# Matmuls of ones ahead of the first projections, other places for one head's key rotation and for weight splits, and another bank for the fourth query

## The reference, cut to what matters

```
x = x + fake_quant(layernorm(x)) @ fake_quant(ctx)            # layer 0, mixing by the context
x = x + mx_ffn(layernorm(x))      # weights rounded to 4 bits, activations to 6, shared exponents per 32
h = layernorm(x)
q = rope(h @ wq)  (32 heads of 128);  k = rope(ctx @ wk), v = ctx @ wv  (8 heads of 128)
x = x + softmax(q k^T / sqrt(128) + mask) v @ wo              # layer 1, attention
x = x + (silu(g * gate(h2)) * u * up(h2)) @ down * d,  h2 = layernorm(x)
```

## Time and profile before

| what | value |
|---|---|
| median of 3 runs | 683.79 us |
| profiled execution: own time / span in the profile | 685.39 us / 683.6 us |
| PE busy, share of the span | 661.1 us, 97% |
| DVE, POOL, ACT busy | 516.4, 474.2, 347.5 us |
| mean granted TensorE clock | 0.998 |

### The profile page before, as it was taken

One profiled execution on the slowest core, in us unless ns is written; L12 is line 12 of the kernel. 1 busy time (PEld: TensorE's weight loads), 2 busy tenths in 40 slices (PEclk: granted clock), 3 DMA queues, 4 the chain that ended last, 5 costly groups with the idle time before them and its releaser, 6 DMA issues.

```text
span 683.6 us, 10829 instructions
## 1 busy us (share of the span) xinstructions
PE 661.1 (97%) x3004; PEld 486.5 (71%) x3004; DVE 516.4 (76%) x1024; ACT 347.5 (51%) x667; POOL 474.2 (69%) x435
## 2 busy tenths in 40 slices
PE   6999999999899999999999999999999998999997
PEld 2344444446667888888888888888888776888886
DVE  5999897986788888888888888888888886621113
ACT  2686324424656656656666666666556653221111
POOL 0688958334698788787787787797688477076661
PEclk9999999999999999999999999999999999999999
DMA  8999775403322222232231131131233012013311
GB/s 317 390 328 245 230 198 133 155 1 121 94 78 78 63 85 70 61 89 64 61 99 54 61 105 48 61 107 46 61 94 121 17 32 92 1 48 102 111 63 62
DMA packets 59147, 72.63 MB, mean 106 GB/s; under 512 B 23152, under 2 KB 31472, under 8 KB 58096
## 3 DMA queue, kind: packets, MB, share of 16 engines
q1 hardware_dynamic: 59120, 72.31, 34.5%
HBM read 58.00 MB, written 9.44 MB: 99 GB/s over the span
## 4 chain that ended last, share of the span: by engine, by line
PE 67%; DVE 14%; POOL 8%; issue 7%; ACT 2%; DMA 1%; SPq 1%; DVEq 0%; ACTq 0%; POOLq 0%
PE ps L683 14%; PE ps L685 14%; PE ps L684 14%; PE ps L751 10%; PE ps L716 6%; PE ps L568 3%; PE ps L542 3%; POOL mx_raw L1148 2%; DMA mx_raw<-in_mxw 1%; DVE ps L1578 1%; PE ps L604 1%; POOL mx_w L1157 1%; DVE mx_amax L1406 1%; POOL prob L1220 1%; DVE stats L1319 1%
## 5 line engine op out<-in xcount | busy, mean ns | idle before, releaser
L1220 POOL TENSOR_SCALAR prob<-prob,rinv 128x512 f32<-128x512 f32 x128 | 90.0, 703 | 73.6 <-DVE rinv L1585 73.5
L1046 ACT ACTIVATE prob<-ps,nmax 128x512 f32<-128x512 f32 x128 | 88.5, 691 | 97.2 <-DVE nmax L1578 96.8
L751 PE MATMUL ps<-xt,wq_sb 128*128 128x512 f32 x384 | 103.2, 393 | 3.6 <-DVE q_cos L1593 2.1
L1057 ACT CAST pT<-ps 128x512 fp32r<-128x512 f32 x128 | 75.2, 588 | 53.0 <-PE ps L716 51.9
L1578 DVE CUSTOM_DVE_ANT_0 ps<-ps,mask_sb 128x512 f32<-128x512 f32 x128 | 88.0, 687 | 6.6 <-PE ps L685 6.1
L1599 DVE TENSOR_TENSOR pT<-ps,pT 128x512 fp32r<-128x512 f32 x128 | 86.5, 675 | 3.0 <-ACT pT L1057 2.0
L751 PEld LDWEIGHTS ps<-xt,wq_sb 128*128 128x128 f32 x384 | 71.6, 188 | 22.3 <-issue 4.9
L716 PE MATMUL ps<-idf,prob 128*128 128x128 f32 x512 | 76.8, 272 | 0.4 <-POOL prob L1220 0.3
L716 PEld LDWEIGHTS ps<-idf,prob 128*128 128x128 f32 x512 | 63.6, 140 | 17.8 <-POOL prob L1220 1.6
L683 PE MATMUL ps<-pT,vt 128*128 128x512 f32 x128 | 60.8, 475 | 0.6 <-DVE pT L1599 0.5
L542 PE MATMUL ps<-ctxT,wk_sb 128*128 128x512 f32 x128 | 58.0, 594 | 0.4 <-ACT v_st L892 0.4
(11 more groups left out here) (179 smaller groups left out, 1548.0 us busy)
## 6 DMA issues: line engine op xcount, KB each, us to landing
mx_raw<-in_mxw SPq DMA_DIRECT2D x8, 1024.0 KB, 8.1
wq_raw<-in_wq SPq DMA_DIRECT2D x32, 256.0 KB, 3.2
wo_raw<-in_wo SPq DMA_DIRECT2D x32, 256.0 KB, 2.7
v_scr<-v_st SPq DMA_DIRECT2D x16, 256.0 KB, 3.7
k_scr<-k_st SPq DMA_DIRECT2D x16, 256.0 KB, 3.5
kr<-k_scr SPq DMA_DIRECT2D x16, 256.0 KB, 2.8
kr_swp<-k_scr SPq DMA_DIRECT2D x32, 128.0 KB, 3.4
vr<-v_scr SPq DMA_DIRECT2D x16, 256.0 KB, 3.3
```

Of the source, the lines that this page charges most:

```text
L751: last = mm(query_bank(H), wq_sb[:, par, l, k], xt[:, r, k], start=(n == 0), stop=(n == 11))
L1046: nc.scalar.activation(prob[:, j], bank(j % 2), ACT.Exp, bias=nmax[:, j:j + 1], scale=-1.0, accum_out=rsum[:, j:j + 1]).then_inc(exps, 1)
L1057: copy(pT[:, v % 2, 0, :, i * P:(i + 1) * P], bank(2 + i % 2).rearrange("p (k c) -> p k c", k=4)).then_inc(ph_ready, 1)
L1220: nc.gpsimd.tensor_scalar(prob[:, i], prob[:, i], rinv[:, i:i + 1], 1.0, ALU.mult, ALU.mult).then_inc(probs, 1)
```

## The change

Eight matmuls of a tile of ones run on PE as soon as the tile is set, into the bank of the first value unit, ahead of `first_values`. On SP's queue slice 1 goes ahead of the four X transfers and slice 2 ahead of the first mx chunk; the second half of wv goes ahead of the first half of the context rows. On ACT the rounding of the rows goes behind the first two value copies and the two first lifts, and those two copies go ahead of the lifts. Head 0's first rotation moves from the projection stage to POOL's place behind the wait for `inter_ready` 3, the second from there to unit -3; their adds, high and low parts move with them: DVE's first add from between two products to just ahead of `add_down(2)`. Query 3 takes bank 7 rather than bank 6, and queries 3 and 4 wait for one `q_cosed` less. The splits of query weights 2 and 3 go ahead of the query product on POOL. The last key unit's matmuls go one right behind `late_keys(3)` and three at unit -1, rather than two at unit -2 and two at unit -1. In `standardise`, `between` is called right behind the first step.

```diff
+WARM = 8
@@ query_bank
-            return bank(7 if isinstance(head, int) and head == 1 else 6)
+            return bank(7 if isinstance(head, int) and head in (1, 3) else 6)
@@ sync
             slice_load(0)
+            slice_load(1)
             for t in range(NT):
                 sp.dma_start(X[:, t], x[t * P:(t + 1) * P]).then_inc(x_in[t], 16)
-            slice_load(1)
+            slice_load(2)
             mx_load(0)
-            slice_load(2)
             slice_load(3)
...
             sp.dma_start(idf[:], ident).then_inc(id_in, 16)
+            sp.dma_start(wv_sb[:, :, 512:1024], ...).then_inc(wv1_in, 16)
             ctx_load(0)
-            sp.dma_start(wv_sb[:, :, 512:1024], ...).then_inc(wv1_in, 16)
@@ tensor
+            def keep_busy():
+
+                pe.wait_ge(consts_ready, 1)
+                for _ in range(WARM):
+                    mm(bank(rotating(STEPS[0][0][0])), ones[:], ones[:].unsqueeze(1).to_broadcast([P, 4, P]), start=True, stop=True)
+            keep_busy()
             first_values()
...
             late_keys(3, range(2, 4))
+            late_keys(4, range(0, 1))
@@ query
-                    first = isinstance(H, int) and H <= 2
-                    after(pe, q_cosed, H // 2 if first else H)
+                    after(pe, q_cosed, H - 1 if isinstance(H, int) and H <= 4 else H)
@@ unit, PE
-                    if isinstance(U, int) and U in (-2, -1) and j == 3:
-                        late_keys(4, range(2 * U + 4, 2 * U + 6))
+                    if isinstance(U, int) and U == -1 and j == 3:
+                        late_keys(4, range(1, 4))
@@ scalar
             rows_scale()
+            copy_values(0, 0)
+            copy_values(1, 0)
             mx_lift(0, 0)
             mx_lift(0, 1)
-            copy_values(0, 0)
-            copy_values(1, 0)
+            rows_round()
...
+            def first_key_high(b):
+                act.wait_ge(key_roped, b + 1)
+                copy(kt[:, 0, b], kr[:, b]).then_inc(kh_ready, 1)
             silu(0)
-            act.wait_ge(key_roped, 1)
-            copy(kt[:, 0, 0], kr[:, 0]).then_inc(kh_ready, 1)
             silu(1)
...
             keep_inter(NT - 1)
+            first_key_high(0)
             copy_keys(*LATE_KEYS[2])
-            act.wait_ge(key_roped, 2)
-            copy(kt[:, 0, 1], kr[:, 1]).then_inc(kh_ready, 1)
             nc.scalar.activation(rsum[:, 0:1], sc[:, 0:1], ACT.Exp, scale=0.0)
...
                         copy(q_swp[64:128], query_bank(H)[0:64]).then_inc(q_swapped, 1)
+                        if isinstance(U, int) and H == 0:
+                            first_key_high(1)
@@ gpsimd
                 if i == L0_AT + 1:
-                    pool.wait_ge(rk_in, 16)
-                    pool.wait_ge(ln_ready, 2 * NT)
-                    first_key_rotate(0)
                     rows_out(0)
                     rows_out(1)
             scale_out(NFULL)
+            pool.wait_ge(rk_in, 16)
             pool.wait_ge(inter_ready, 3)
-            first_key_rotate(1)
+            first_key_rotate(0)
...
+                    if isinstance(U, int) and U in (-2, -1) and j == 0:
+                        query_split(U, u, g)
                     if j == 0 and within(U + 2, NH):
...
-                    if j == 1 and within(U + 4, NH):
-                        (wait for wq_in and q_sums, split)
+                    if j == 1 and not (isinstance(U, int) and U in (-2, -1)):
+                        query_split(U, u, g)
+                    if isinstance(U, int) and U == -3 and j == 1:
+                        first_key_rotate(1)
@@ vector
                 chain(ln, ts(var, meanvar[:, lo:hi, 1], 1e-5, None, ALU.add))
+                if between:
+                    between()
...
-                    if n == 1 and between:
-                        between()
...
             inter_product(0, 1)
-            first_key_add(0)
             inter_product(0, 2)
...
                 inter_quantise(t)
                 add_down(t - 2)
+            first_key_add(0)
             add_down(NT - 2)
...
-            first_key_add(1)
             rows_low()
             first_key_low(0)
-            first_key_low(1)
+            first_key_add(1)
             dve.wait_ge(mask_in, 16)
...
                            ropeQ[:, 0]..., ALU.mult).then_inc(q_cosed, 1)
+                        if isinstance(U, int) and H == 0:
+                            first_key_low(1)
```

More of the change, by code:

```diff
@@ L377, in _ @@
             sp.dma_start(idf[:], ident).then_inc(id_in, 16)
+            sp.dma_start(wv_sb[:, :, 512:1024], wv[:, 512:1024].rearrange("(k p) c -> p k c", p=P)).then_inc(wv1_in, 16)
             ctx_load(0)
-            sp.dma_start(wv_sb[:, :, 512:1024], wv[:, 512:1024].rearrange("(k p) c -> p k c", p=P)).then_inc(wv1_in, 16)
             k_load(1)
@@ L906, in rows_scale, with rows_round @@
                 nc.scalar.activation(rows, rows, ACT.Identity, bias=sc[:, 1:2], scale=sx[:, 0:1]).then_inc(q1_scaled, 1)
+            def rows_round():
+                rows = xhat[:].rearrange("p t d -> p (t d)")
                 act.wait_ge(q1_scaled, 1)
@@ L1211, in _, with query_split @@
             split(wq_sb[:, 0, 0], wq_sb[:, 0, 1], wq_raw[:, 0], wqh_ready, wq_split, 1)
+            def query_split(U, u, g):
+                H, par = U + 4, u % 2
+                if within(H, NH):
+                    pool.wait_ge(wq_in[par], 16 * (g * 2 + (u + 4) // 2 + 1))
+                    after(pool, q_sums, H - 1)
+                    split(wq_sb[:, par, 0], wq_sb[:, par, 1], wq_raw[:, par], wqh_ready, wq_split, H + 1)
             def unit(U, u, g):
```

## The result

The changed kernel takes 685.15 us (median of 18 executions, 684.48 to 686.21); the kernel before, timed beside it, 683.75 (18, 682.84 to 685.13). The ratio is 1.0020, with a 95% interval of 1.0014 to 1.0027: slower by some 1.4 us, where 1.45 us faster was forecast, and outside the range of 680.2 to 684.2. The profiled execution of the changed kernel took 685.39 us, with a span of 683.6 and a mean granted clock of 0.997; the span of before's was the same 683.6, but at 685.39 us that was a high execution of its kernel, above all 18 of those timed. So the two traces are compared stretch by stretch, not end to end.

The account below looks back on a forecast made before the run. It took PE as busy throughout the attention loop, with DVE as full between 18 and 77 us. Terms +0.2 + 0 - 1.15 - 0.5 = -1.45 us took 683.79 to 682.3 us; own range 681.3 to 683.0, 8-in-10 range 680.2 to 684.2.

Parts of the forecast that it names:

- Projection stage: First stretch, up to PE's value unit at 76.70: DVE's chain sets it, later X costs +0.2 us (ends 0 and +0.5).
- So DVE loses about 0.4 of the 1.4 us (lift end 21.0 against 20.60): Projection stage: X lands 1.4 us later, but DVE needed ACT's first lift only at 20.60, so loses about 0.4 us.
- It is swallowed: DVE's 0.4 us loss vanishes in its 0.68 us idle at 63.42 if the transfer ending that idle comes no later.
- The lead of PE and the ones: Projection stage: PE leads by 2.1 us, but DVE's chain hides it; lead and matmuls of ones costed at 0.
- Rival A: PE's projection-stage lead survives: the 0.2 us loss goes, 0.5 to 2.1 us gained, 680.0 to 681.6 us; chance 0.15.
- Rival C: Slower: two value copies hold ACT's first lift if slice 3 lands late, delaying DVE's chain; 685.2 us or more; chance 0.07.
- FFN: Layer 0's FFN: DVE's key add moves behind POOL's int_q product, ahead of `add_down(2)`; 0 us (ends -0.3 and +0.5).
- Start of attention: PE's first queries and scores: gaps filled, bank 7 removes a wait; -1.15 us (gain 0.85 to 1.55).
- rival B: No difference that can be told: POOL-DVE locks delay head 0's rope chain, or clock falls; 683.3 us (682.5 to 684.5); chance 0.30.
- End of attention: PE's wait until 581.51 for DVE's low part: PE starts 0.75 us sooner; -0.5 us (ends -0.4 and -0.9).
- now at about 583.7: End of attention: PE turns the layer norm's rows at about 583.7 instead of 584.1.
- The sum: Whole kernel: +0.2 + 0 - 1.15 - 0.5 = -1.45 us, giving 682.3 us; forecast's chance 0.48.

Follow-up runs that it names:

- e2: Kernel before with only SP's queue order changed: slice 1 ahead of the X transfers, slice 2 ahead of mx chunk 0; 685.59 us, ratio 1.0018 to before.
- e12: Changed kernel with the second chunk's exponent on DVE moved behind the first instruction of the first rounding; 684.38 us, ratio 0.9998 to before.
- e7: Changed kernel without the matmuls of ones; 685.34 us, ratio 1.0015 to before.
- e5: Changed kernel with the front of before: SP's order, ACT's order and first matmuls put back; 683.96 us, ratio 0.9990 to before.
- e10: e9 with the last six late-key instructions moved between the second and third query on PE; 682.46 us, ratio 0.9970 to before.
- e11: e6 with six more matmuls of ones in PE's stall near 174 us; 683.64 us, ratio 0.9989 to before.
- e8: Kernel before with only the last low part moved, `between()` called right behind `var_eps`; 684.02 us, ratio 0.9996 to before.
- e4: Changed kernel with DVE's first key add moved behind the layer norm's last rows; 684.36 us, ratio 0.9998 to before.
- e6: e5 with the first key add also put behind the layer norm's last turn; 683.50 us, ratio 0.9986 to before.
- e1: Kernel before again, nothing changed; 684.36 us, ratio 0.9996 to before.
- e3: Changed kernel with the four X transfers back ahead of slice 1; 684.56 us, ratio 1.0005 to before.
- e9: e6 with POOL's weight splits of the third and fourth query back behind the queries' sines; 685.09 us, ratio 1.0009 to before.

## Why the prediction was wrong, by its own steps

- **Projection stage: +0.2 forecast, 1.1 measured by e2, 1.4 for the whole front.** The mechanism (X one slice later, 1.4 us) came as forecast: statistics at 7.9, first lift at 19.9 for 20.0. The step that failed is "So DVE loses about 0.4 of the 1.4 us (lift end 21.0 against 20.60)". It compared two times and left out the instruction that stands between the second reduce and the rounding: an exponent of 0.20 us. POOL's scaling, which had moved by the same 1.4 us, now runs over it, and DVE stands for 1.67 us. The prediction used the lock between DVE and POOL for the key add, and not here; e12, which moves this one instruction, gets 0.8 us back (685.15 less 684.38), and its profile has the forecast 0.4 us left. The Trainium skill, "SBUF — State Buffer", section "Who interferes with whom", says that a DVE instruction in a mode that takes both of its ports shuts out GpSimd or is shut out by it, whichever came second, and names `tensor_scalar` among those that can enter such a mode; this exponent is one, and the ends (21.81 and 21.76 us) bear that out.
- **"It is swallowed" at 63.42.** DVE's idle time there did go: its reduce starts at 63.77, 0.35 late. But POOL, whose product DVE waits for a few instructions on, was 1.1 us late on its own account, and the whole 1.1 us was back at 69.96 us (68.83 before). An idle moment on one of two engines that wait for each other in turn absorbed nothing here:

```profile
63.77 2.27 DVE L1427 TENSOR_REDUCE mx_amax<-mx_raw 128x64 f32<-128x2048 f32 x1
...
69.96 0.20 DVE L1433 TENSOR_SCALAR mx_e<-mx_amax 128x64 uint32<-128x64 uint32 x1 [1.80 <-POOL mx_w L1173]
```

- **The lead of PE and the ones: 0, as forecast.** PE led by 2.3 us at the first keys and had spent it by 66.85 us; e7 shows the ones at nothing. Rival A did not happen. Rival C's time came without its mechanism: the two value copies were through by 18.7 us, and the first lift then waited 1.20 us for POOL.
- **FFN: 0, as forecast** (46.66 against 46.72). The key add took 2.73 us and `add_down(2)` came right behind it.
- **Start of attention: -1.15 forecast, 0.1 to 0.5 measured.** Counted from layer 0's first matmul, the third score did come 1.08 us sooner (64.84 us behind it for 65.92), by the chain that was priced: the first exponent stands at 174.3 us in before's frame, where 174.1 to 174.8 was given. (The first score came 1.9 us sooner, where 1.5 was expected.) The step that failed is to take that for the gain of the stage. Two things took most of it back by the first product. In e5, which kept its clock, DVE's low part of the third query at 178.90 met POOL's scaling of a probability (178.81, 0.70 us) and took 1.15 us instead of the 0.69 of before; that is 0.46 of the 0.54 us by which e5's gain, counted from the turn, falls from 1.03 us at the third score to 0.49 at the product. No run moves this pair on purpose, but in e10 the same low part comes 0.10 us ahead of the scaling: it takes 0.69 us, POOL's takes 1.15, and the gain is 1.47 us at the third score and still 1.38 at the product. DVE in before, e5 and e10:

```profile
179.46 0.69 DVE L1608 TENSOR_TENSOR qt<-q_cos,qt 128x512 fp32r<-128x512 f32 x1 [1.34 <-ACT qt L1082]
178.90 1.15 DVE L1629 TENSOR_TENSOR qt<-q_cos,qt 128x512 fp32r<-128x512 f32 x1 [1.34 <-ACT qt L1097]
177.54 0.69 DVE L1627 TENSOR_TENSOR qt<-q_cos,qt 128x512 fp32r<-128x512 f32 x1 [1.34 <-ACT qt L1097]
```

  POOL in the same three:

```profile
178.91 0.70 POOL L1220 TENSOR_SCALAR prob<-prob,rinv 128x512 f32<-128x512 f32 x1
178.81 0.70 POOL L1240 TENSOR_SCALAR prob<-prob,rinv 128x512 f32<-128x512 f32 x1
177.64 1.15 POOL L1240 TENSOR_SCALAR prob<-prob,rinv 128x512 f32<-128x512 f32 x1
```

  The changed kernel's profile has the same meeting (179.60, 1.14 us), and its clock fell behind the stall of 1.91 us (granted 0.76, four query matmuls in 1.67 us instead of 1.17), so 0.1 was left. The prediction named this fall under rival B and put the stall at 1.6 us. The wait of the first sine behind a split, priced right, was avoidable: with the splits and the late keys moved, e10 gets 0.8 to 0.9 us more (30.26 against 31.15 in e5 and 31.10 in e11).
- **End of attention: -0.5 forecast, -0.8 or +0.1 measured, by the execution.** The step "now at about 583.7" against 584.1 held only because before's six matmuls there ran at the lower clock in the profile. Where the clock stays up the layer norm bounds both, and there is nothing to gain.
- **The sum.** At full clock the terms are +1.1 to +1.4, 0, -0.5 and +0.1: +0.7 to +1.0. The executions at a mean clock of 0.999 or more have medians of 683.9 (before, e8's group) and 684.8 (changed): +0.9, though across groups; e7 against before in its group is +0.87. The interval of the measured ratio, +1.0 to +1.9 us, begins there. What makes up the rest of the +1.4 stays open: before's median lay 0.4 to 0.8 us lower in that timing than in the later ones, and how often the clock falls in each kernel (in half of the changed one's executions, at another place than before's) was not controlled.

## What to carry to other kernels

When a transfer is put behind another, follow what it releases on every engine, and lay the new times of each engine pair that locks the other over each other, instruction by instruction: here a 0.2 us instruction that slid under a 1.9 us one cost DVE 0.7 us, where the late transfer alone cost it 0.4. A lead on an engine was worth nothing where the next meeting point was set by another, and a wait that looked like slack was none, since the partner's chain was late too. Before costing an edit at a stall, ask whether the profiled execution ran that stretch at full clock.

## What the runs showed of the hardware

- The granted clock fell behind idle times of PE of 1.9 us (changed, e4, e6, e12), 2.15 us (before, e1), and 2.28 us (e3), in some executions and not in others: with the same 1.9 us it stayed at 1.00 in the profiles of e3, e5 and e7, with 2.16 us in that of e2, and with 2.60 us in that of e9. With the 1.9 us filled by six bf16 matmuls (1.47 us, leaving 0.60 us idle), none of 11 executions had a mean clock below 0.999.
- A fall of the clock cost 0.94 us of End (7.49 against 6.55), but only 0.3 to 0.4 us of Start, where other engines set the pace.
- DVE's first statistics on X started between 5.68 and 7.53 us in eight profiles with before's queue order. In three of them the exponent took 0.41 (e6, the one at 7.53), 0.57 (e5, where the last part of X came only at 9.23) and 0.32 us (e9): even the kernel before stands at the edge of this meeting. In its own profile 0.15 us are to spare between the scaling's end and the exponent, in e1's 0.23.
